# A routed-expert layer on one core: token pairs in a new order, router logits side by side, and h transposed back only behind them

## The reference, cut to what matters

```python
h = (x - mean(x, -1)) * rsqrt(var(x, -1) + 1e-5) * ln_g + ln_b       # x is 8 x 512 x 256
h = (h - mean(h, 1)) * rsqrt(var(h, 1) + 1e-8)                       # over the 512 tokens of a batch row
gamma, beta = small_mlp(subj_emb[ids]); h = h * gamma + beta         # gamma through softplus
probs = softmax(h @ router_w)                                        # 8 experts
gates, idx = top_k(probs, 2); gates = gates / gates.sum(-1)
y = sum over the two chosen experts of gate * (relu(h @ w1[e] + b1[e]) @ w2[e] + b2[e])
out = x + y
```

## Time and profile before

| | |
|---|---|
| median of 3 runs | 494.72 us (493.55 to 495.49) |
| the profiled execution's own time | 495.7 us |
| its span in the trace | 493.6 us |
| last h modulated (L402 ends) | 49.05 us |
| counts on PE (L611) | 57.59 us |
| first gather (L323) | 66.72 us |
| first expert matmul (L687) | 71.53 us |
| PE busy in the span | 94% |

### The profile page before, as it was taken

One profiled execution on the slowest core, in us unless ns is written; L12 is line 12 of the kernel. 1 busy time (PEld: TensorE's weight loads), 2 busy tenths in 40 slices (PEclk: granted clock), 3 DMA queues, 4 the chain that ended last, 5 costly groups with the idle time before them and its releaser, 6 DMA issues.

```text
span 493.6 us, 15842 instructions
## 1 busy us (share of the span) xinstructions
PE 463.4 (94%) x5700; PEld 418.1 (85%) x5700; DVE 384.0 (78%) x1439; ACT 277.9 (56%) x838; POOL 224.4 (45%) x189
## 2 busy tenths in 40 slices
PE   7899768999999999999999999999999999999990
PEld 5754448899999999999999999999899999999990
DVE  4898778899888878878888888888888877777640
ACT  2467526566565566555566665566556555555440
POOL 0643221555454455554554454454555444444422
PEclk8789958999999999999999999999999999999997
DMA  8943673344444434434444443444444332322321
GB/s 315 407 143 129 214 180 130 81 101 112 91 88 92 95 87 90 119 87 89 98 89 91 113 92 88 93 93 93 109 96 88 53 49 46 55 45 46 53 26 21
DMA packets 37819, 51.67 MB, mean 105 GB/s; under 512 B 8064, under 2 KB 29840, under 8 KB 37488
## 3 DMA queue, kind: packets, MB, share of 16 engines
q0 software_dynamic: 13632, 18.91, 22.5%
q1 hardware_dynamic: 21488, 31.14, 19.5%
q10 hardware_dynamic: 2624, 0.62, 0.6%
HBM read 36.74 MB, written 18.11 MB: 111 GB/s over the span
## 4 chain that ended last, share of the span: by engine, by line
PE 80%; DVE 8%; DMA 5%; ACT 3%; issue 2%; POOL 1%; SPq 0%; ACTq 0%; DVEq 0%; POOLq 0%
PE bank L687 37%; PE bank L694 34%; PE bank L642 3%; DMA out_rows<-yout,tok 3%; PE bank L636 2%; PE bank L506 1%; DVE tns L784 1%; DMA par<-in_params 1%; PE bank L515 1%; ACT hid L461 1%; DVE bns L760 1%; DMA hg<-h_rows,tok 1%; DVE hidlo L1084 1%; DVE wlo L1069 0%; POOL whi L287 0%
## 5 line engine op out<-in xcount | busy, mean ns | idle before, releaser
L461 ACT ACTIVATE hid<-bank,par 128x128 f32<-128x128 f32 x568 | 162.2, 368 | 164.7 <-PE bank L687 162.9
L687 PE MATMUL bank<-hThi,whi 128*128 128x128 f16 x1136 | 189.4, 220 | 5.2 <-DVE hTlo L1074 1.6
L687 PE MATMUL bank<-hTlo,whi 128*128 128x128 f16 x1136 | 189.3, 220 | 0.0
L331 POOL DMA_INDIRECT out_rows<-yout,tok x71 | 119.6, 1684 | 110.5 <-ACT yout L473 85.7
L687 PE MATMUL bank<-hThi,wlo 128*128 128x128 f16 x1136 | 157.1, 220 | 0.0
L694 PE MATMUL bank<-whi,hidlo 128*128 (+1 forms) x568 | 154.8, 273 | 0.0
L694 PE MATMUL bank<-whi,hidhi 128*128 (+1 forms) x568 | 154.8, 273 | 0.0
L694 PE MATMUL bank<-wlo,hidhi 128*128 (+1 forms) x568 | 154.8, 273 | 0.0
L323 POOL DMA_INDIRECT hg<-h_rows,tok x71 | 83.5, 1176 | 112.7 <-DVE tok L1060 102.2
L687 PEld LDWEIGHTS bank<-hThi,whi 128*128 (+1 forms) x1136 | 111.6, 99 | 14.8 <-issue 7.1
L687 PEld LDWEIGHTS bank<-hTlo,whi 128*128 (+1 forms) x1136 | 111.9, 98 | 5.5
(11 more groups left out here) (170 smaller groups left out, 458.2 us busy)
## 6 DMA issues: line engine op xcount, KB each, us to landing
stage<-in_exp_w SPq DMA_DIRECT2D x64, 256.0 KB
whi<-in_x SPq DMA_DIRECT2D x8, 512.0 KB, 8.4
out_rows<-in_x SPq DMA_DIRECT2D x8, 512.0 KB, 16.1
h_rows<-wlo SPq DMA_DIRECT2D x8, 512.0 KB, 3.7
hg<-h_rows,tok POOLq DMA_INDIRECT x71
out_rows<-yout,tok POOLq DMA_INDIRECT x71
b2row<-in_exp_b SPq DMA_DIRECT2D x1, 1024.0 KB, 20.6
par<-in_params SPq DMA_DIRECT2D x1, 517.5 KB, 6.2
```

The lines of the kernel that those rows point to most:

```text
L331: gp.indirect_dma_start(out=out, out_offset=bass.IndirectOffsetOnAxis(ap=tok[:, t:t + 1], axis=0), in_=yout[:, t % 2, :], in_offset=None, ...
L461: ins = S(hid32[:, par, c * P:(c + 1) * P], bk_hid[half][:, (c - 4 * half) * P:(c - 4 * half + 1) * P], ACT.Relu, bias=vcol[:, bass.ds(e * ...
L687: hid_ins = MM(o, lhs[w, k], h[:, par, k * P:(k + 1) * P], start=(n == 0), stop=(n == 3 * KD - 1))
```

## The change

Four things at once, all in the first part:

- **Order by pairs.** DVE takes the token statistics of pair 1 (b = 2, 3) ahead of the style network's steps and those of b = 4 to 7 earlier too, so POOL can normalise earlier. The bank ring of `transposes` has six banks instead of five. The product of gamma and ln_g is taken once (`gg`) and not for each pair. `modulate(7)` moves from ACT to DVE (`tensor_scalar`, fires `last_h_modulated`).
- **Logits side by side.** `logits(b0, b1)` runs over k outside and b inside: b = 0 to 3 in one go behind `transposes(6, 1)`, then 4 and 5, then 6 and 7. Before there was a go for each b, between the transposes.
- **Back behind the logits.** All 16 `back` and `half_rows` now stand behind `modulate(6)`; in between stand only the logits and their copies. `back(7, 0)` and `back(7, 1)` stand behind the counts. SP stores h of b = 6 and 7 behind its four gate stores.
- **Selection and gates.** The steps of `select` are written out one by one and those of part 0 and part 1 interleave. The exponential of the second largest logit, plus 1, is the sum of the two (`two_sum` on DVE), so POOL needs two operations for each part and not five. `selh` is written with the expert outside.

The diff, cut to its core:

```diff
-        bk_T = banks[0:5]
-        bk_back = (banks[7], banks[5])
-        bk_log = (banks[6], banks[1])
+        bk_T = banks[0:6]
+        bk_log = (banks[6], banks[4])
+        def bk_back(i):
+            return banks[5] if i % 2 == 1 else banks[7]
...
+            for b in range(6):
+                store_h(b)
             sp_.wait_ge(s_comb, 1)
             for b in range(BP):
                 store_gates(sp_, b)
+            for b in range(6, B):
+                store_h(b)
...
                 gp.wait_ge(s_exp, part + 1)
+                gp.wait_ge(s_rec, part + 1)
+                gp.tensor_tensor(exr3, ex3, m8[:, 5, j0:j1].unsqueeze(2).broadcast_to([P, n, E]), ALU.mult).then_inc(s_gp, 1)
+                gp.wait_ge(s_gp, part + 1)
                 gp.wait_ge(s_sel, part + 1)
-                link(gp.tensor_tensor(ex3, ex3, chosen3, ALU.mult))
-                link(gp.tensor_tensor(half, ex3[:, :, 0:4], ex3[:, :, 4:8], ALU.add))
-                link(gp.tensor_tensor(quarter, half[:, :, 0:2], half[:, :, 2:4], ALU.add))
...
+                gp.tensor_tensor(comb3, exr3, chosen3, ALU.mult).then_inc(s_comb, 1)
...
             def router_exp(part, j0, j1):
-                act.wait_ge(s_d, part + 1)
+                act.wait_ge(s_m2, part + 1)
+                S(m8[:, 4, j0:j1], m8[:, 2, j0:j1], ACT.Exp)
                 S(ex[:, j0 * E:j1 * E], d1[:, j0 * E:j1 * E], ACT.Exp).then_inc(s_exp, 1)
...
-            def logits(b):
-                pe.wait_ge(s_h2, 2 * b + 2 if b < BP else max(2 * b + 2, 12))
+            def logits(b0, b1):
+                pe.wait_ge(s_h2, min(2 * b1, 14))
+                if b1 == B:
+                    pe.wait_ge(s_h2v, KD)
                 for k in range(KD):
+                    for b in range(b0, b1):
...
             transposes(3, 0)
             transposes(3, 1)
-            logits(0)
+            warm(4)
             transposes(4, 0)
-            back(0, 0)
-            logits(1)
-            back(0, 1)
             transposes(4, 1)
+            warm(6)
             transposes(5, 0)
-            back(1, 0)
             transposes(5, 1)
-            logits(2)
-            back(1, 1)
+            warm(6)
             transposes(6, 0)
-            logits(3)
             transposes(6, 1)
-            back(2, 0)
+            logits(0, BP)
             transposes(7, 0)
             transposes(7, 1)
...
             ins.then_inc(s_ccol, 1)
+            back(7, 0)
...
+            back(7, 1)
-            warm(10, 1)
+            warm(4, 1)
...
+            def modulate(b):
+                ve.wait_ge(s_tr, 2 * b + 2)
+                ve.wait_ge(s_mc, b // 2 + 1)
+                for k in range(KD):
+                    at = b * KD + k
+                    V.tensor_scalar(hT[b][:, k * T:(k + 1) * T], bk_T[at % 6][:, :], hA[:, at:at + 1], hB[:, at:at + 1],
+                                    ALU.mult, ALU.add).then_inc(s_h2v, 1)
```

## The result

The changed kernel takes 499.41 us (median of 4 runs, 499.13 to 500.2). Beside it, on the same chip, the kernel before took 494.47 us. The ratio is 1.0102, 95% interval 1.0083 to 1.0122: **slower by 5 us, 1.0%**. The forecast was 493.4 with a range to 496.0, so the time fell outside it, on the other side. The profiled execution of after took 499.13 us against 495.7 for that of before.

A forecast was written before the change was run, and what follows sets the result against it. PE bounds the long second part, whose start follows the first gather, held by ACT's gate stores. Last modulation 45.5 plus 19.9 puts the gather at 65.4 against 66.72, 1.3 less: median 493.4 us, range 490.9 to 496.0.

The forecast's parts named there:

- M: Moment when the last h is modulated; forecast 45.5 us, 3.5 earlier than the 49.05 of the kernel before.
- The sum's road: From the last modulation through copies, counts and ACT's gate stores to the first gather: 19.9 us, against 17.67 before.
- the signs that the prediction named for being wrong: Counts follow selection at once, gather waits for other than ACT's stores, or second part's length changes by over 1 us.
- SP's list agrees: SP's list behind M: h of b = 6 and 7 until 15.2 to 15.9, agreeing with gather at M + 19.9.
- The other end of the range: Halves at 0.75 each, or stores of b = 6 and 7 landing last: gather at M + 21.
- The price at the start: Moments and four more statistics on DVE delay pair 0's modulation_ready from 24.66 to 25.1.
- L: End of the logits of b = 0 to 3: 38.6, 39.4 or 40.9 us by the clock; M = L + 5.4.
- its two cases with the clock down: PE's clock falls in two holes: L at 39.4 or 40.9, M at 44.8 or 46.3; midway taken, 45.5.
- Capped at two: Rival: logits overlap only two abreast, L 1.5 later, M 47.0, time 494.9; chance 0.12.
- The clock holds: Rival: PE's clock holds or returns by 34, four logits abreast, M 44.0, time 491.9; chance 0.20.
- Clock down behind M: Rival: lower clock slows logits and transposes of halves behind M, 3.2 slower, 497.9; chance 0.09.
- Does not bring M forward: Rival: DVE is the bound all the way, M = 49, 2.2 slower, 496.9; chance 0.04.

The follow-up runs named there:

- e11: Changed kernel with h of b = 6 and 7 not stored, rows of x written early in their place: 496.28 us, ratio 1.0038.
- e1: Kernel before, with SP storing no row of h until all of h is modulated: 496.61 us, ratio 1.0035.
- e6: Changed kernel with POOL's normalisation of b = 6 and 7 cut to 8 columns of one of four tiles: 497.89 us, ratio 1.0056.
- e7: Changed kernel with more filler matmuls in PE's two holes, 16 to 40 and 6 to 40: 496.86 us, ratio 1.0039.
- e10: Kernel before with more filler matmuls only, 10 to 24 and 6 to 26: 493.94 us, ratio 0.9994.
- e4: Changed kernel with seven of 16 halves copied ahead of M, h stores ahead of SP's gates, all halves ahead of counts: 492.55 us, ratio 0.9957.

## Why the prediction was wrong

**The bound of before was read rightly.** The prediction put the gather 6.25 behind ACT's gate stores and carried that distance over. The last of them landed at 65.7, and the gather followed 1.0 later. Where no store of h is late, in e11, the distance is 6.4 and the gather stands at M + 19.1, against the forecast's M + 19.9. The sum's road holds for that kernel. One of the signs that the prediction named for being wrong came true in after: the gather waits for something else than ACT's stores.

**The term that failed: stores of h behind the gates.** The prediction listed SP's times ("h of b = 6 and 7 until 15.2 to 15.9", that is M + 15.9) and then wrote that SP's list agrees. There it compared issue times with the gather: to M + 15.9 the landing has to be added, which makes M + 19.2 with the 3.3 that a store took in before at best and M + 22.2 with the 6.3 that it took here, and then the 0.9 from the landing to the gather. Measured: issued at M + 15.6 (63.12), landed at M + 21.9, gather at M + 22.8. The issue time was right to 0.3. What was missing is the landing, and that it is longer in full DMA engines: the 4.2 MB that before had gone out from 36 us on now left behind M, in one piece, and the landings of the eight stores grew from 3.4 for the first to 6.3 for the last. The other end of the range, M + 21 "if the stores of b = 6 and 7 land last", named the mechanism and priced it 1.8 too low, and the sum was kept without it. e11 shows it: without these two, 3.1 us are gone.

**M, too early by 2.0.** By its own steps:
- Pair 0 was ready at 26.03, forecast 25.1: 0.9 late. The price at the start was put at 0.4 (24.66 to 25.1) and is 1.4, and that against a sample of before in which pair 0 was itself 1.2 later than in e1. It is not the clock's: in all eleven profiles of the new order pair 0 was ready 18.0 to 18.1 behind DVE's first statistics, whether the clock came back at 16.7 or at 20.6. Which of the steps that DVE now has ahead of it cost more was not tried.
- Pair 1 at 34.66, forecast 32.7: another 1.0. e6 has the cause, 1.2 us, POOL's work in the small steps. The prediction took their length from the last pair of before, when POOL was idle (0.16 in the earlier trace rows at 32.02 and 0.41 at 24.25 stood side by side there, and it should have asked why).
- Pair 2 was 5.25 behind pair 1, forecast 4.6 to 5.2, and pair 3 at L + 3.95, forecast L + 3.9: right to 0.05.
- M at L + 5.6, forecast L + 5.4. `modulate(7)` on DVE was 1.53 for two and not 1.3: wrong by 0.2, where the text had named 0.15.
- The clock fell in both holes, as forecast, to its lower level (0.50 from 26 to 32, 0.56 to 0.58 from 36 to 40), and cost 1.4 (e7). The forecast took half of it, the middle between its two cases with the clock down.

And the base was 49.05, the M of an execution with the clock down from 25.6 to 29 and until 18.8. At the upper level from 20 us on it is 46.8 to 47.4 (e10, e1). The prediction compared a forecast for after with one sample of before, and 1.7 us of what M could gain were that sample's.

**Right.** Four logits abreast in 1.92, forecast 2.2. The last half copied at M + 13.4, forecast 13.6, and the counts at M + 10.8, forecast 11.1, behind `back(6, 1)`. The second part, 422.4 against 422.1.

**The rivals.** "Capped at two" fell, by the row of 1.92. "The clock holds" did not happen by itself. "Clock down behind M" did not happen: the clock was at its upper level from 40 to 70, while the time went beyond that rival's 497.9. "Does not bring M forward" was given 0.04 and 496.9; at equal clock about a third of the gain came (0.9 to 1.2 of 3.5). No rival had the late stores, which decided: for slower than before the chance was 0.10.

**The parts, as far as the runs separate them.** Against before, between the two profiles: M -1.53, the copies between M and the counts +2.30, counts to gather +2.85, together +3.62. The last is what e11 takes out, 3.7 between the profiles (counts + 12.0 to + 8.3) and 3.1 in the medians. It is more than 2.85 because ACT's gates start 1.9 behind the counts in e11 and started 2.9 behind them in before. The medians have 4.9 in all: the two profiled executions differ by 3.43, that of before lay 1.23 above its median and that of after 0.28 below its own.

## What to carry to other kernels

When work is pushed behind a point, push its stores along in the sum: write down for each store when it is issued, what is in the DMA engines by then, and when it lands, and compare landings with landings. Check the releaser that a timeline names against the kernel's own waits: here it named a column of tokens that the first gather does not need, while the last landing stood the same 0.9 to 1.0 ahead of the gather in every kernel. A wait that passes by its name for the bound can send a repair to the wrong engine. A copy that fits into a gap ahead of the point costs nothing there and a full turn of two engines behind it.

## What the runs showed of the hardware

- DVE steps of 128x4 elements took 0.16 us with POOL idle; of pair 1's eight, four took 0.35 to 0.50 while POOL ran its tensor-scalar passes over 128x256; taking POOL's work away brought them back to 0.16 (e6).
- A store of 512 KB landed 3.3 us (median) behind its issue with eight spread over 24 us (e4), 5.6 with eight issued in 9.7 us (e1), and 6.3 as the last of its kernel in after and 6.8 in e7.
- The first gather started 0.9 to 1.0 us behind the last landing of the stores in all fourteen profiles.
- Two executions of the same first part had the granted clock at different levels (0.79 from 22 to 30 in the profile of before, 1.00 in that of e1, and 0.80 against 1.00 from 18 to 20), and M 1.7 us apart, 1.2 of it by 25 us. What sets the level in one execution and not in the other was not settled.
- With 24 and 26 fillers on the kernel before, the runs lay between 492.17 and 496.67, wider than the 493.55 to 495.83 of the kernel before beside them.
